# A causal mask moved from TensorE's matmuls to GpSimd's select on the probabilities

## The reference

```python
q = (x @ Wqa @ Wqb).reshape(b, s, 16, 8)             # 16 heads of width 8
kv = (x @ Wkva @ Wkvb).reshape(b, s, 4, 8, 2)        # 4 groups of keys and values
q, k = _rope(q), _rope(k)                            # each group serves 4 heads
scores = jnp.einsum('bqhd,bkhd->bhqk', q, k) * scale
causal = jnp.triu(jnp.ones((s, s), dtype=bool), k=1)
scores = jnp.where(causal[None, None], -jnp.inf, scores)
w = jax.nn.softmax(scores, axis=-1)
out = jnp.einsum('bhqk,bkhd->bqhd', w, v).reshape(b, s, E)
return out @ Wout + bout
```

## Time and profile before

| | us |
|---|---|
| median of the runs | 1230.65 |
| the profiled execution, its own time | 1230.85 |
| its span | 1229.0 |
| TensorE busy | 1099.2 |
| VectorE busy | 928.7 |
| ScalarE busy | 742.2 |
| GpSimd busy | 186.8 |
| second pass, first scores to last values | 485 to 922 |

### The profile page before, as it was taken

One profiled execution on the slowest core, in us unless ns is written; L12 is line 12 of the kernel. 1 busy time (PEld: TensorE's weight loads), 2 busy tenths in 40 slices (PEclk: granted clock), 3 DMA queues, 4 the chain that ended last, 5 costly groups with the idle time before them and its releaser, 6 DMA issues.

```text
span 1229.0 us, 18062 instructions
## 1 busy us (share of the span) xinstructions
PE 1099.2 (89%) x5956; PEld 613.7 (50%) x5971; DVE 928.7 (76%) x1803; ACT 742.2 (60%) x1088; POOL 186.8 (15%) x144
## 2 busy tenths in 40 slices
PE   3897668899999677999999999999996999999998
PEld 2333235577777523333333232222225788888886
DVE  5599998455655576799899999999606788888885
ACT  2635426688788522445566666666784666666664
POOL 0000001499899900100000000000000000000000
PEclk9999777899999876999999999999995899999999
DMA  6000001799997314200000000000000211111001
GB/s 172 1 0 1 1 0 48 158 203 203 209 202 172 132 26 97 51 2 2 2 1 2 1 1 2 1 2 1 1 1 1 97 60 60 60 60 60 1 1 35
DMA packets 39521, 65.44 MB, mean 53 GB/s; under 512 B 14622, under 2 KB 30782, under 8 KB 34126
## 3 DMA queue, kind: packets, MB, share of 16 engines
q1 hardware_dynamic: 39446, 64.43, 21.5%
HBM read 61.17 MB, written 3.11 MB: 52 GB/s over the span
## 4 chain that ended last, share of the span: by engine, by line
PE 62%; DVE 26%; ACT 5%; issue 4%; POOL 2%; DMA 1%; SPq 0%; DVEq 0%; POOLq 0%; ACTq 0%
PE ps L929 10%; PE ps L930 10%; PE ps L931 10%; PE ps L1142 9%; PE ps L1071 7%; DVE arena_b L1902 6%; PE ps L1120 5%; DVE arena_b L1649 3%; PE ps L1127 2%; POOL parts L741 2%; PE ps L1084 2%; DVE arena_b L1830 1%; PE ps L791 1%; DVE arena_b L1663 1%; ACT arena_b L1462 1%
## 5 line engine op out<-in xcount | busy, mean ns | idle before, releaser
L1462 ACT ACTIVATE arena_b<-ps 128x1024 f32<-128x1024 f32 (+3 forms) x320 | 273.8, 894 | 154.2 <-PE ps L1120 130.6
L929 PE MATMUL ps<-parts 128*128 128x512 f32 x640 | 253.2, 396 | 10.1 <-POOL parts L741 7.6
L930 PE MATMUL ps<-parts 128*128 128x512 f32 x640 | 250.0, 391 | 0.0
L931 PE MATMUL ps<-parts 128*128 128x512 f32 x640 | 249.8, 390 | 0.0
L1902 DVE TENSOR_REDUCE arena_b<-ps 128x1 f32<-128x512 f32 x384 | 238.3, 681 | 9.8 <-PE ps L1071 8.4
L1071 PE MATMUL ps<-arena_a 48*128 48x512 bf16 (+7 forms) x820 | 179.0, 311 | 12.8 <-DVE arena_b L1902 4.5
L741 POOL TENSOR_TENSOR parts<-arena_b,parts 128x512 fp32r<-128x512 f32 x128 | 166.7, 1311 | 62.7 <-ACT parts L1392 58.1
L1142 PE MATMUL ps<-arena_b 128*32 128x512 f32 (+3 forms) x1280 | 151.1, 544 | 0.0
L1830 DVE SCALAR_TENSOR_TENSOR arena_b<-ps,arena_a 128x512 f32<-128x512 f32 x128 | 87.0, 688 | 80.5 <-PE ps L931 80.4
L1120 PE MATMUL ps<-arena_a 50*128 50x512 bf16 (+3 forms) x832 | 139.3, 311 | 7.9 <-DMA arena_a<-arena_b 4.0
L1071 PEld LDWEIGHTS ps<-arena_a 48*128 48x128 bf16 (+1 forms) x832 | 60.3, 96 | 170.7 <-DVE arena_b L1902 104.7
(11 more groups left out here) (270 smaller groups left out, 1140.1 us busy)
## 6 DMA issues: line engine op xcount, KB each, us to landing
arena_a<-root_weights SPq DMA_DIRECT2D x60, 512.0 KB, 6.6
arena_b<-expert_weights SPq DMA_DIRECT2D x7, 1024.0 KB, 6.1
arena_a<-q_parts SPq DMA_DIRECT2D x36, 64.0 KB
wslot<-in_L_ffn_up_w SPq DMA_DIRECT2D x8, 256.0 KB, 7.0
wslot<-in_L_ffn_down_w SPq DMA_DIRECT2D x8, 256.0 KB, 7.6
wslot<-in_L_ffn_w_gate SPq DMA_DIRECT2D x8, 256.0 KB, 2.9
wslot<-in_L_ffn_w_up SPq DMA_DIRECT2D x8, 256.0 KB, 3.2
wslot<-in_L_ffn_w_down SPq DMA_DIRECT2D x8, 256.0 KB, 3.8
```

Of the source, the lines that this page charges most:

```text
L929: mm(bank, w(0), x(0), start=start, stop=False)
L930: mm(bank, w(0), x(1), start=False, stop=False)
L931: return mm(bank, w(1), x(0), start=False, stop=stop)
L1462: a(probs[:, s % 2, 2 * pair:2 * pair + 2, off:CW], ps[:, 2 + 2 * pair:4 + 2 * pair, off:CW], ACT.Exp, scale=scale).then_inc(p2_exp, 1)
```

## The change

The mask of the second pass leaves TensorE. `sum_scores` now issues one matmul a head over all of the columns from `off` on. GpSimd, after the exponential of each pair of a diagonal step, runs one `affine_select` on the 128x128 corners of its two heads in `probs`, in place: probabilities with a query before the key become 0. It raises `p2_mask`, and `values(s)` waits for it in diagonal steps (`MASKED[s]` counts the selects, two a step). The output bias's addition, on the same engine, moves behind the 32 selects of the c = 0 items and waits no longer for the maxima.

```diff
+        MASKED, masked = {}, 0
+        for s, (n, j) in enumerate(STEPS):
+            if j >= TPC * ITEMS[n][0]:
+                masked += 2
+                MASKED[s] = masked
+        BIAS_AT = 2 * TPC * next(n for n, (c, _) in enumerate(ITEMS) if c > 0)
...
-            pool.wait_ge(nm_ready, G1)
-            pool.wait_ge(wo1_ready, 1)
-            g.tensor_tensor(xt[:, :, :], xt[:, :, :], bo1[:, :].unsqueeze(1).broadcast_to([P, NT, D]), ALU.add)\
-                .then_inc(bias_ready, 1)
+            for s, (n, j) in enumerate(STEPS):
+                off = (j - TPC * ITEMS[n][0]) * P
+                if off < 0:
+                    continue
+                for pair in range(2):
+                    pool.wait_ge(p2_exp, 2 * s + pair + 1)
+                    corner = probs[:, s % 2, 2 * pair:2 * pair + 2, off:off + P]
+                    g.affine_select(corner, corner, [[0, 2], [1, P]], ALU.is_ge, 0.0, 0, -1).then_inc(p2_mask, 1)
+                if MASKED[s] == BIAS_AT:
+                    pool.wait_ge(wo1_ready, 1)
+                    g.tensor_tensor(xt[:, :, :], xt[:, :, :], bo1[:, :].unsqueeze(1).broadcast_to([P, NT, D]), ALU.add)\
+                        .then_inc(bias_ready, 1)
...
-                full = off + P if j >= TPC * c else off
-
-                def part(i, lo, hi, stop):
+                for i in range(2):
                     r = slice(STRIP * i, STRIP * i + MROWS)
-                    return mm(ps[:, 2 + 2 * pair + i, lo:hi], kst[r, i, g, j * P:(j + 1) * P],
-                              qst[r, c, g, pair, lo:hi], start=True, stop=stop)
-
-                if full > off:
-                    for i in range(2):
-                        part(i, off, full, False)
-                    for i in range(2):
-                        last = mm(ps[:, 2 + 2 * pair + i, off:full], identb[:, :], maskkq[:, :], start=False, stop=True)
-                if full < CW:
-                    for i in range(2):
-                        last = part(i, full, CW, True)
+                    last = mm(ps[:, 2 + 2 * pair + i, off:CW], kst[r, i, g, j * P:(j + 1) * P],
+                              qst[r, c, g, pair, off:CW], start=True, stop=True)
                 last.then_inc(p2_mm, 1)
...
                 pe.wait_ge(p2_exp, 2 * s + 2)
+                if j >= TPC * c:
+                    pe.wait_ge(p2_mask, MASKED[s])
```

More of the change, by code:

```diff
@@ L390, in adaln_two_layers @@
         ld_q = [sem(f"ld_q{c}") for c in range(NC)]
+        p2_mask = sem("p2_mask")
         kzero = sem("kzero")
```

## The result

The kernel after takes 1219.91 us (median of 16 runs, 1215.53 to 1229.22), the kernel before beside it 1233.49 (16 runs, 1227.23 to 1238.95). The ratio is 0.9912 with a 95% interval of 0.9883 to 0.9941: 10.9 us less, 7 to 14; the means of the same runs, 1232.86 and 1221.99, are as far apart, the medians 13.6. That is faster by just under 1%, so within what I had called no change (41 in 100), where the forecast was 15.4 us less (1216) and the likeliest case was faster by over 1% (46).

A forecast was written before the change was run, and what follows sets the result against it. TensorE and VectorE nearly full in middle items, so removed TensorE time counts only where VectorE idles. 12.2 + 2.0 + 1.2 + 0 = 15.4 us off 1230.85 gives 1216 us (63 in 100); range 1208 to 1223, reaching on to 1238.

The forecast's parts named there:

- The mechanism: Second pass's diagonal steps: TensorE sheds 2.4 us an item, worth only what VectorE has idle there.
- Items 1 to 13: Second attention's middle work items: 16.7 us of VectorE idle, 13.6 after deductions, 90% realized, so 12.2 us gained.
- item 9 and its neighbours: Sign of being right: these second-pass items each 0.7 to 1.1 us shorter, VectorE's busy time unchanged.
- Item 0: First work item of the second pass, at clock 0.70 with VectorE idle 4.7 us: 2.0 us gained.
- item 14: Second-to-last work item: 1.5 us of VectorE idle, 1.3 on offer, 1.2 us gained; last two steps 0.
- Item 15: Last work item, filled by ScalarE's exponentials: earlier scores and later values called equal, gain 0.
- The select: GpSimd's mask in diagonal steps: 0.78 us each, range 0.42 to 1.8, 128 in all, hidden where slots stand between.
- VectorE beside GpSimd: Selects beside VectorE's work: no charge, as reductions read PSUM; only small subtractions would suffer.
- slow select: Rival, 16 in 100: above 1.2 us a select everything waits for GpSimd; 1228 us at 1.31, 1275 at 1.8.
- The colder clock: Rival, 13 in 100: TensorE's clock falls in diagonal steps; one in each of items 0 to 6 gives 1226 us.
- Masks hidden anyway: Rival, 8 in 100: VectorE is already the limit in the second pass, gain 0 to 5 us, 1228 us.
- The bias addition: GpSimd's 4.51 us addition, moved behind item 3's last diagonal step: stays hidden with 3 us to spare.

The follow-up runs named there:

- e5: Kernel before with VectorE's first-pass reductions over half of their columns; 1209.76 us in one profiled execution.
- e6: Kernel after with VectorE's first-pass reductions over half of their columns; 1186.63 us in one profiled execution.
- first profile after: First profiled execution of the kernel after, nothing changed; 1225.44 us.
- second profile after: Kernel after run once more, unchanged, for another profiled execution; 1224.28 us.
- e8: Kernel before with one idle GpSimd select added on the zeroed padding of hT at program start; median 1236.48 us, ratio to before 1.000.
- e2: Kernel after without selects or the wait for them, second-pass mask left out, bias addition back in its old place; 1216.02 us.
- e3: Kernel after with each select over all 512 columns of its two heads instead of the corner; 1247.24 us.
- e9: Kernel after with seven filler matmuls in TensorE's idle stretch ahead of the pass; median 1220.92 us, ratio to before 0.9895.
- e11_both: Kernel after with four filler matmuls in TensorE's idle stretch and the first pass's mask matmuls removed; 1201.8 us, ratio to before 0.9717.
- e10: Kernel before with seven filler matmuls in TensorE's idle stretch ahead of the pass; median 1230.14 us, ratio to before 0.998.
- e1: Kernel before with diagonal scores as one matmul a head and the mask matmuls kept behind them; 1230.72 us in one profiled execution.

## Why the prediction was right or wrong

**The mechanism, right.** TensorE sheds work that is only worth what VectorE has idle there. `e5` and `e6` show it: 22.2 us instead of 7.8 when VectorE's reductions take 0.42 us instead of 0.68.

**Items 1 to 13, mis-sized: 12.2 forecast, 7.8 measured.** The step that failed is the one from the earlier trace rows to the gain: 16.7 us of idle time, less 3.1, times 0.9. The windows of the earlier trace rows, drawn in the same way in the kernel after, add up to this:

```profile
sum 143.11, PE 130.51 PEld 38.16 DVE 133.81 ACT 83.69 POOL 38.46; mean PE 10.04 PEld 2.94 DVE 10.29 ACT 6.44 POOL 2.96
```

They are 8.4 us shorter, with 9.3 us of VectorE's idle time left, where the forecast had left 4.5 (16.7 less 12.2). Of their 52 steps those that got shorter gave 11.2 us, near the forecast; others got longer and took 2.7 back; and outside of the windows the items got longer by another 0.6. So what I had wrong is that a step's gain stays. I took VectorE's idle time as recoverable where it stands, and two things are against that. VectorE's floor is not its busy time in the window but the reductions that the step must get through: the fourth step was already full, and when the three ahead of it were shortened it grew by 0.12 (that it had been living on their delay is my reading). And what a step gains is given back at the next place where VectorE's work is late anyway. In items 11 and 12 the step with the maxima's work went from 2.89 to 3.38 and from 2.78 to 3.20 us, and these items gained 0.4 and 0.1 us where items 8, 9, 10 and 13 gained 0.5 to 0.8; in item 4 a step went from 2.73 to 3.21 behind one that had lost 0.87; item 3 gained nothing. In `e6`, with a less busy VectorE, these steps take 2.2 to 2.3 us. My statement that "item 9 and its neighbours" shorten by 0.7 to 1.1 us holds for item 9 (0.78) and item 8 (0.65) only about; item 10 gained 0.64.

**Item 0: 2.0 forecast, 1.3 and 1.7 measured (1.8 and 2.2 from its first scores on); item 14: 1.2 forecast, 1.05 and 1.19.** Nearly right.

**Item 15: 0 forecast, 0.6 to 1.9 measured.** I had set the earlier scores against later values, with a select of 0.78 us. It is 0.409, and 0.6 us remain as the change's own gain. The larger gain came when the clock did not fall at the item's start: in the kernel before the value step at 894 us took 2.79 us at clock 0.50, in the first profile after 1.53 at 1.00. The second profile after has the fall (0.50 at 891 to 895 us) and gained only 0.6. `e8`, with its masks on TensorE, has no fall there and takes 29.23 us, 0.6 more than the first profile after and 1.3 less than the kernel before. So the other 1.3 us are the clock, and luck of the profiled execution.

**The select: 0.78 taken, 0.41 measured**, just under the lower end of the range (0.42) and by the memset's row, not the addition's. It costs next to nothing where slots cover it: 0.4 us in items 1 to 13 beside no select at all (`e2`), and 1.2 in items 14 and 15. No loading time shows at its first use: the first exponential ends at 494.14 us, and the first select takes 0.41 from 494.21.

**VectorE beside GpSimd, right for the reductions.** They take 681 ns as before. Four small instructions on SBUF stand out in the trace after, each beside a select: one subtraction with two inputs and three casts with one. The slowest of each:

```profile
758.82 0.42 DVE L1956 TENSOR_TENSOR arena_a<-arena_b,arena_a 128x16 bf16<-128x16 f32 x1
...
800.61 0.38 DVE L1955 CAST arena_a<-arena_b 128x16 bf16<-128x16 f32 x1
```

The other two casts take 0.37 (at 500.81) and 0.34 (883.13). The median of either line is 0.18 us, and before none of the 32 passed 0.18. So I was wrong to say that only subtractions would suffer; together the four are longer by 0.8 us. Another subtraction, at 511.85, lay beside a select for all of its 0.18 us and was not slowed. The Trainium skill, GPSIMD Engine Reference, section 8, names VectorE's instructions with two SBUF inputs, and beside them those in a 2-port perf mode, which I had left out. The subtraction at 758.82 agrees with the first; whether the casts ran in such a mode no trace here shows.

**The rivals.** The slow select did not happen. At 1.46 us a pair it cost about what I had put on it; at 1.05 it was hidden in items 4 to 10, and `e3` still took 1247 us. The colder clock did not happen in the pass. "Masks hidden anyway" was half true: of some 31 us that thirteen items shed (an estimate, 2.4 each), 7.8 arrived, where I had left 12.2.

**The bias addition** moved behind the selects of item 3 and stayed hidden; no wait of VectorE on it shows.

**The verdict.** The gain of 10.9 us is 4.5 short of the forecast, and the mis-sized term alone is 4.4; item 0's shortfall and item 15's gain of 0.6 at the same clock come near to cancelling.

## What to carry to other kernels

Where two engines are nearly full, cut the time into steps and ask of each whose step it is: here the work removed counted for four fifths in steps that were mostly its engine's (the first pass's masks, 11.9 of 14.8 us) and for a quarter in the others (the second pass's masks, 7.8 of 31). Ask also whether a mask is needed at all: the first pass's was not, and leaving it out gave more than moving the other. Put the other engine's floor into the sum as the instructions that it must get through in each step, and then look one step on, where that engine's own work comes late in any case. Compare profiled executions stretch by stretch: 6.9 us of the difference between these two profiles lay in a stretch that the change does not touch, and were the clock's.

## What the runs showed of the hardware that I had not expected

- One select on a 128x256 f32 tile takes 0.409 us, on 128x1024 1.047 us: about 0.20 us and 0.83 ns an element of a partition, the rate of GpSimd's memset (0.85) and not of its two-input addition (2.1).
- An idle stretch of TensorE of 3.9 us was followed by a clock of 0.50 for 6.8 us in five profiles, one of 3.6 to 3.7 us by 23.9 us of it in six others, with the same matmuls behind it and TensorE busy all the while (5.00 of 5.00 us from 225 to 230). Filled with matmuls whose result nobody reads, it was followed by no fall in three of three profiles. The timed runs then spread over 4.1 us (`e9`), 3.6 (`e11_both`) and 9.3 (`e10`), against 13.7 in the kernel after and 11.7 before; with 6 to 10 runs against 16 that is a hint, no more.
- Two mask matmuls of 128x128 behind a pair of scores cost TensorE 0.31 us, splitting the pair's scores in two 0.02 (`e1`).
- A cast of 128x16 from SBUF to SBUF took up to 0.38 us beside a select and 0.18 alone, a subtraction up to 0.42.
- Longer waits of TensorE on a neighbour went with a fall of its clock: `e3` lost 3 to 5 us in each of four items, with the clock at 0.50 for a stretch of 7 to 10 us in or just ahead of each.
